# A two-layer graph attention kernel: the last chunk's pairs are taken one row later, its chain of small steps stays in the first twelve half pairs

## What is computed

```
h = relu(layernorm(x));  x = x + hyperbolic_graph_conv(h, adj)       # "L0_gnn"
h = relu(layernorm(x))
for beta in (beta1, beta2):                                           # "L1_gnn", two layers
    n = h / |h|
    s = where(adj > 0, beta * (n @ n.T), -1e9)
    h = leaky_relu(softmax(s) @ h)                                    # slope 0.3
x = x + h
```

## Time and profile before

| | before |
|---|---|
| median of 3 executions | 963.98 us (963.15 to 964.41) |
| the profiled execution, its own time | 963.64 us |
| span of its trace | 962.0 us |
| PE busy | 926.9 us, 96% of the span |
| PEld busy | 692.1 us, 72% |
| DVE busy | 792.5 us, 82% |
| ACT busy | 538.0 us, 56% |
| chain that ended last | PE 86%, ACT 6%, DVE 5% |
| DMA | 207.26 MB, mean 215 GB/s |

### The profile page before, as it was taken

How to read it: one execution, slowest core, us unless ns; L and a number is a source line. 1 busy time by engine, 2 the same in 40 slices (tenths; PEclk the granted TensorE clock), 3 DMA queues, 4 the chain that set the end, 5 groups by cost and what they waited for, 6 DMA issues and landing times.

```text
span 962.0 us, 22931 instructions
## 1 busy us (share of the span) xinstructions
PE 926.9 (96%) x9016; PEld 692.1 (72%) x9016; DVE 792.5 (82%) x1980; ACT 538.0 (56%) x867; POOL 7.2 (1%) x20
## 2 busy tenths in 40 slices
PE   7799999999997999999999999999999999999996
PEld 6644444444445878888888888778888888888886
DVE  7874778777789887978989898998788787888888
ACT  7802222232337766657656667796575565656564
POOL 0000000000000000000000000000000000000000
PEclk9999999999999999999999999999999999999998
DMA  8368888888851555455655545545455555565631
GB/s 298 154 222 289 283 298 293 279 286 283 293 180 57 232 196 210 186 202 198 249 195 212 220 180 216 210 160 201 177 219 219 232 206 201 220 228 194 259 144 37
DMA packets 30419, 207.26 MB, mean 215 GB/s; under 512 B 3632, under 2 KB 4784, under 8 KB 5744
## 3 DMA queue, kind: packets, MB, share of 16 engines
q1 hardware_dynamic: 28752, 203.70, 58.5%
q0 software_dynamic: 560, 1.84, 0.5%
q10 hardware_dynamic: 1008, 0.33, 0.1%
HBM read 203.75 MB, written 2.10 MB: 214 GB/s over the span
## 4 chain that ended last, share of the span: by engine, by line
PE 86%; ACT 6%; DVE 5%; issue 2%; DMA 0%; DVEq 0%; ACTq 0%
PE acc_ps L496 23%; PE s_ps L649 18%; PE s_ps L635 10%; PE acc_ps L707 6%; PE acc_ps L703 6%; PE acc_ps L705 6%; PE acc_ps L680 5%; PE acc_ps L676 5%; PE acc_ps L678 5%; ACT work L1078 1%; ACT set L800 1%; DVE work L1742 1%; PE s_ps L477 1%; ACT xt L822 1%; DVE work L1750 1%
## 5 line engine op out<-in xcount | busy, mean ns | idle before, releaser
L1078 ACT ACTIVATE work<-s_ps,beta_bias,beta_scale 128x1024 f32<-128x1024 f32 x144 | 173.5, 1205 | 212.2 <-PE s_ps L649 212.2
L496 PE MATMUL acc_ps<-ring,set 128*128 128x512 f32 x512 | 222.1, 592 | 1.6 <-DVE set L1348 1.6
L1760 DVE SCALAR_TENSOR_TENSOR h_all<-ring,s_ps 128x1024 f32<-128x1024 f32 x112 | 136.6, 1220 | 65.3 <-PE s_ps L635 63.9
L496 PEld LDWEIGHTS acc_ps<-ring,set 128*128 128x128 f32 x512 | 96.2, 190 | 117.5 <-issue 115.6
L1742 DVE TENSOR_TENSOR work<-work 128x1024 f16<-128x1024 f32 x96 | 132.7, 1382 | 5.4 <-ACT work L1088 5.4
L1088 ACT ACTIVATE work<-work 128x1024 f16<-128x1024 f32 x96 | 131.5, 1370 | 3.0
L1750 DVE SCALAR_TENSOR_TENSOR work<-ring,work 128x1024 f32<-128x1024 f32 x96 | 116.9, 1218 | 0.0
L649 PE MATMUL s_ps<-xt 128*128 128x512 f16 x432 | 105.4, 379 | 4.1 <-ACT work L1078 3.3
L649 PE MATMUL s_ps<-set 128*128 128x512 f16 x432 | 105.0, 379 | 0.5 <-ACT work L1078 0.5
L703 PE MATMUL acc_ps<-src,work 128*128 128x129 f16 x576 | 102.5, 219 | 2.0 <-DVE work L1750 2.0
L707 PE MATMUL acc_ps<-src,work 128*128 128x129 f16 x576 | 102.8, 222 | 0.0
(11 more groups left out here) (279 smaller groups left out, 1737.9 us busy)
## 6 DMA issues: line engine op xcount, KB each, us to landing
ring<-in_adj_t SPq DMA_DIRECT2D x192, 1024.0 KB, 5.0
x_sb<-in_x SPq DMA_DIRECT2D x4, 512.0 KB, 7.2
out<-x_sb POOLq DMA_DIRECT2D x7, 256.0 KB, 2.7
out<-x_sb SPq DMA_DIRECT2D x1, 256.0 KB, 2.7
w<-in_layer ACTq DMA_DIRECT2D x2, 64.0 KB, 8.2
w<-in_embed ACTq DMA_DIRECT2D x1, 64.0 KB, 4.5
eb<-in_embed_bias ACTq DMA_DIRECT2D x1, 64.0 KB, 6.9
lb<-in_layer_bias ACTq DMA_DIRECT2D x1, 64.0 KB, 7.9
```

Of the source, the lines that this page charges most:

```text
L496: last = nc.tensor.matmul(agg, v_sb[:, jb, :], ring[:, k, b, :], start=jb == 0, stop=jb == NB - 1)
L1078: nc.scalar.activation(values[x.n % VR], score_ps, ACT.Exp, bias=beta_bias[:, x.la:x.la + 1], scale=beta_scale[:, x.la:x.la + 1]).then_inc ...
L1760: V.scalar_tensor_tensor(turned[x.off % MR].rearrange("p (b j) -> p b j", b=CB), ring[:, x.mir_tile % AR, :, ds(x.h * HB * P, HB * P)], 0. ...
```

## The change

The order of the first layer's pairs becomes (0,0), ... (0,6), (1,1), ... (1,7), (7,0), (2,2), and then as before. Row 0 is thus left open after its first fourteen half pairs: its own sums are copied out to `mirror_sums` by a new ACT step (`own_kept`), row 1 is done (half pairs 14 to 27), and the missing pair is done as (7,0) (half pairs 28 and 29), where the rows of 7 are the "own" ones and those of 0 the mirrored. A new DVE step (`late_total`) makes row 0's total from the kept and the mirrored sum and adds the own part to what is kept for row 7. Before, row 0 ended at half pair 15 and row 1 at 29; now row 1 ends at 27 and row 0 at 29. Chunk 7's columns are turned at slot 24 instead of 12; the first half pair that needs them is 26 instead of 14. The column sums must wait until the bank of own sums is opened for row 1, and go to slots 18 to 23 and 27. `SLOTS_PER_PAUSE` is 1, so the chain of chunk 7 has its twelve pieces in the same slots 1 to 12 as before. The second layer's order is unchanged.

```
+        LATE = NC - 1
+        kept_seg = add_seg(0, 0, range(LATE), None, 0)
+        seg = add_seg(0, 1, range(1, NC), 0, 1)
+        rows_of.append(Row(0, 1, seg.first, seg.last))
+        late_seg = add_seg(0, LATE, (0,), None, 2)
+        rows_of.append(Row(0, 0, kept_seg.first, late_seg.last))
+        LATE_ROW = 1
...
-        LAST_CHUNK_AT = 12
-        turned_at = {LAST_CHUNK_AT: (0, NC - 1), **{rows_of[a].last + (11 if a == 5 else 10): (1, a) for a in range(NC)}}
...
+        LAST_CHUNK_AT = 24
+        order_of = {(r.la, r.a): i for i, r in enumerate(rows_of)}
+        turned_at = {LAST_CHUNK_AT: (0, NC - 1), **{r.last + (11 if r.a == 5 else 10): (1, r.a) for r in rows_of[:NC]}}
...
-        SUMS_AT_OF = {4: (0, 1), 5: (2,), 6: (3,), 7: (4,), 8: (5,), 14: (6,), SUMS_AT: (7,)}
...
+        SUMS_AT_LA = (rows_of[0].last, LAYER + 2 * NC - 1)
+        SUMS_AT_OF = {SUMS_AT_LA[0] - 11 + i: c for i, c in {2: (0, 1), 3: (2,), 4: (3,), 5: (4,), 6: (5,), 7: (6,),
+                                                             11: (7,)}.items()}
...
+        SLOTS_PER_PAUSE = 1
...
+                    if x.pair == late_pair:
+                        last = nc.tensor.matmul(mir_ps[:, x.h, o], tiny[:, :], sums_parts, start=False, stop=True)
...
-                if x.n == r.first and x.row != LAST_ROW:
-                    wait(pe, total_made, x.row)
...
+                if x.n == seg.first and seg.row != LAST_ROW:
+                    wait(pe, total_made, seg.opens_after)
...
+            def own_kept():
+
+                act.wait_ge(own_added, kept_seg.last + 1)
+                nc.scalar.activation(mirror_sums[:, 0:CB, :].rearrange("p (k b) w -> p k (b w)", k=2), own_ps, ACT.Copy)\
+                    .then_inc(total_made, 1)
...
+                if x.la == 0 and (x.a, x.b) == (1, NC - 1):
+                    V.tensor_copy(kept, mir_ps).then_inc(flushed, 1)
+                    return
...
+            def late_total():
...
+                dve.wait_ge(mir_added, half[late_seg.last].off + 1)
+                dve.wait_ge(total_made, 2)
+                dve.wait_ge(flushed, late_pair)
+                V.tensor_tensor(both, kept, mir_ps, ALU.add).then_inc(flushed, 1)
+                dve.wait_ge(own_added, late_seg.last + 1)
+                V.tensor_tensor(late, late, own_ps, ALU.add).then_inc(total_made, 1)
+                dve.wait_ge(flushed, late_pair + 1)
+                V.reciprocal(fin[:, LATE_ROW % 2, 0, :], sums_in[:, :, F]).then_inc(inverse_made, 1)
```

More of the change, by code:

```diff
@@ L290, in __call__ @@
                 self.eng.wait_ge(self.s, self.base + self.n)
-        Half = namedtuple("Half", "la a b h n off pair row own_tile mir_tile")
+        Half = namedtuple("Half", "la a b h n off pair seg own_tile mir_tile")
+        Seg = namedtuple("Seg", "first last row opens_after")
         Row = namedtuple("Row", "la a first last")
-        half, rows_of, tile_of = [], [], []
+        half, segs, rows_of, tile_of = [], [], [], []
         off_count = [0]
[L296 to L308, removed]
@@ new lines, in add_seg @@
+        def add_seg(la, a, bs, row, opens_after):
+            first = len(half)
+            for b in bs:
+                own_tile = len(tile_of)
+                tile_of.append((b, a, len(half) + 1, None))
+                if b != a:
+                    tile_of.append((a, b, len(half) + 1, off_count[0] + 1))
+                for h in range(2):
+                    off = off_count[0] if b != a else None
+                    off_count[0] += b != a
+                    half.append(Half(la, a, b, h, len(half), off, off // 2 if b != a else None, len(segs),
+                                     own_tile, own_tile + 1))
+            segs.append(Seg(first, len(half) - 1, row, opens_after))
+            return segs[-1]
@@ new lines, in build @@
+        LATE = NC - 1
[5 more added lines that the diff above has]
+        LATE_ROW = 1
+        for a in range(2, NC):
+            seg = add_seg(0, a, range(a, NC), a, a + 1)
+            rows_of.append(Row(0, a, seg.first, seg.last))
+        for a in range(NC):
+            seg = add_seg(1, a, range(a, NC), NC + a, NC + 1 + a)
+            rows_of.append(Row(1, a, seg.first, seg.last))
@@ L313, in build, with flushes_before, rows_summed_to, totals_to @@
         row_ending = {r.last: i for i, r in enumerate(rows_of)}
-        LAST_CHUNK_AT = 12
-        turned_at = {LAST_CHUNK_AT: (0, NC - 1), **{rows_of[a].last + (11 if a == 5 else 10): (1, a) for a in range(NC)}}
-        columns_before = {n: sum(m < n for m in turned_at) for n in turned_at}
-        SUMS_AT = 2 * NC - 1
-        SUMS_AT_OF = {4: (0, 1), 5: (2,), 6: (3,), 7: (4,), 8: (5,), 14: (6,), SUMS_AT: (7,)}
+        late_pair = half[late_seg.first].pair
+        def flushes_before(r):
+            return max([x.pair + 1 for x in half if x.off is not None and x.la == r.la and x.b == r.a], default=0)
+        def rows_summed_to(i):
+            return i + 1 - (i >= LATE_ROW)
+        def totals_to(i):
+            return i + 2
+        LAST_CHUNK_AT = 24
+        order_of = {(r.la, r.a): i for i, r in enumerate(rows_of)}
+        turned_at = {LAST_CHUNK_AT: (0, NC - 1), **{r.last + (11 if r.a == 5 else 10): (1, r.a) for r in rows_of[:NC]}}
+        columns_before = {n: sum(m < n for m in turned_at) for n in turned_at}
+        def turn_of(la, c):
+            return order_of[0, c] if la else c
+        SUMS_AT_LA = (rows_of[0].last, LAYER + 2 * NC - 1)
+        SUMS_AT_OF = {SUMS_AT_LA[0] - 11 + i: c for i, c in {2: (0, 1), 3: (2,), 4: (3,), 5: (4,), 6: (5,), 7: (6,),
+                                                             11: (7,)}.items()}
+        SUMS_AT_OF.update({LAYER + i: c for i, c in {4: (0, 1), 5: (2,), 6: (3,), 7: (4,), 8: (5,), 14: (6,),
+                                                     2 * NC - 1: (7,)}.items()})
         def tile_wait(eng, q):
@@ L680, in mirrored_sum @@
                         last = nc.tensor.matmul(mir_ps[:, x.h, o], w[:, WORD_LO, col], src[x.la][:, q, F:AW],
-                                                start=False, stop=ib == CB - 1)
+                                                start=False, stop=ib == CB - 1 and x.pair != late_pair)
+                    if x.pair == late_pair:
+                        last = nc.tensor.matmul(mir_ps[:, x.h, o], tiny[:, :], sums_parts, start=False, stop=True)
                 last.then_inc(mir_added, 1)
@@ L687, in own_sum @@
             def own_sum(x):
-                r = rows_of[x.row]
+                seg = segs[x.seg]
                 pe.wait_ge(own_made, x.n + 1)
@@ L701, in own_sum @@
                         col, q = ds(u * CH + ib * P, P), x.b * CB + x.h * HB + u
-                        opens = x.n == r.first and u == 0 and ib % 2 == 0
+                        opens = x.n == seg.first and u == 0 and ib % 2 == 0
                         nc.tensor.matmul(own_ps[:, ib // 2, ds(ib % 2 * PW, PW)], w[:, WORD_HI, col],
@@ L710, in own_sum @@
                 last.then_inc(own_added, 1)
-                if x.n == r.last:
+                if x.n == seg.last and seg.row is not None:
                     pe.wait_ge(sums_split, 4 * x.la + 4)
@@ L729, in columns_turned @@
                 la, c = turned_at[n]
-                rows = rows_n[c % 2] if la else t3
-                pe.wait_ge(xn_ready[la], c + 1)
+                rows = rows_n[turn_of(la, c) % 2] if la else t3
+                pe.wait_ge(xn_ready[la], turn_of(la, c) + 1)
                 pe.wait_ge(raised, n + 1)
@@ L747, in pairs @@
                         own_sum(done)
-                    if n % LAYER in SUMS_AT_OF and n < NH:
-                        for c in SUMS_AT_OF[n % LAYER]:
+                    if n in SUMS_AT_OF:
+                        for c in SUMS_AT_OF[n]:
                             rows_summed(n // LAYER, c)
@@ L1141, in slot @@
             def slot(n):
[L1142 removed]
+                if n - 1 in SUMS_AT_LA:
                     la = n // LAYER
@@ L1154, in slot @@
                 first = x and x.off is not None and x.h == 1 and x.a == 0
-                if i is not None and rows_of[i].a == 0:
+                own_leaves = n - 4 == kept_seg.last or (i is not None and i == NC)
+                if n - 4 == kept_seg.last:
+                    own_kept()
+                elif i == NC:
                     first_total(i)
@@ L1160, in slot @@
                     raise_scores(at(n))
-                if i is not None and first:
+                if own_leaves and first:
                     first_flush(x)
@@ L1174, in between @@
             def between(i):
-                slot(i + 1)
+                for n in range(SLOTS_PER_PAUSE * i + 1, SLOTS_PER_PAUSE * (i + 1) + 1):
+                    slot(n)
             def pairs():
                 last_chunk(between)
-                for n in range(PAUSES + 1, NH + 4):
+                for n in range(SLOTS_PER_PAUSE * PAUSES + 1, NH + 4):
                     slot(n)
@@ L1857, in slot @@
                 x = at(n - 4)
```

(13 more changed lines are left out.)

40 lines of the change are left out of this document (23 added, 17 removed).

## The result

| | before | after |
|---|---|---|
| median, 5 executions each | 963.16 us (962.91 to 964.41) | 967.51 us (967.32 to 968.31) |
| ratio after / before | | 1.0039, 95% interval 1.0027 to 1.0051 |
| the profiled execution, its own time | 963.64 us | 967.32 us |
| span of its trace | 962.0 us | 965.8 us |
| PE / PEld / DVE / ACT busy | 926.9 / 692.1 / 792.5 / 538.0 us | 926.7 / 691.2 / 793.8 / 537.8 us |

The account below looks back on a forecast made before the run. DVE, with ACT in slots 10 and 11, bounds slots 4 to 11; PE leads afterwards. Sums +2.7 and row ends +1.2 give +3.9 on 963.98: 967.9 us, own range 966.9 to 968.8, 8-in-10 range 965.6 to 969.8.

Parts of the forecast that it names:

- What bounds the kernel: Slots 4 to 11 lose 3.9 us; DVE bounds slots 4 to 9, DVE with ACT 10 and 11; PE leads afterwards.
- the 0.84: Slots 8 and 9: 0.84 us over PE's own work, put down to DVE.
- Part 1: Chunk 7's turn moved from slot 12 to 24: gain 0; the chain's pieces and the 3.9 us of stalls stay.
- Part 2: Six column sums leave slots 4 to 8, where DVE leads, for full slots 18 to 22: +2.7 us.
- Part 3: own_kept, open row, late pair: 0; row 1's total 2.0 us into slot 31, needed at 2.7, 0.7 to spare.
- Rival C: Slot 31's total over 0.7 us late, or row pieces of slots 34 to 38 add up: 970.4 us, chance 9%.
- Part 4: Two row ends interleave in slots 33 to 38: PE waits 0.9 us for ACT's exp, 0.3 for low halves, +1.2.
- 0.3 in slot 38: Slot 38: PE wants DVE's low halves at 27.4, they are done at 27.7, so it waits 0.3 us.
- The sum: Whole kernel: +2.7 + 1.2 = +3.9 us, on a median of 963.98 us.
- The signs: Slots 4 to 11 unmoved to 0.3 us, 18 to 22 longer, 12 at 4.93, idle before slot 35, 3.9 later from 40.
- A: PE led slots 4 to 8, so the stalls there dissolve without the sums: 961.3 us, chance 4%.
- B: Row-end cost hidden and half the sums' price got back in slots 4 to 8: +1.35, 965.3 us, chance 12%.

Follow-up runs that it names:

- the first experiment: The changed kernel with the column sums of chunks 0 to 5 issued in slots 4 to 8 again: 964.98 us, ratio 1.0013.
- the second: The kernel before, its order of pairs kept, with the first layer's column sums of chunks 0 to 5 in slots 12 and 13: 966.21 us, ratio 1.0028.
- flush-first run: The changed kernel with the first six small steps of row 0's scale moved behind the flush at the start of slot 37: 967.35 us, ratio 1.0035.
- first two runs: Column sums of chunks 0 to 5 early again in the changed kernel, 964.98 us; the same sums late in the kernel before, 966.21 us.
- two staggered versions: Changed kernel, chain pieces two slots apart, DVE's and ACT's pauses staggered: 961.69 us; the same with row 0's steps four slots later: 960.46 us.
- the staggered version: The changed kernel with SLOTS_PER_PAUSE = 2 and pauses no longer alike on DVE and ACT: 961.69 us, ratio 0.9981.
- the one with row 0 later: The staggered version with row 0's steps behind its total four slots later as well: 960.46 us, ratio 0.9966.
- first three experiments: Changed kernel with sums early, 964.98 us; kernel before with sums late, 966.21 us; changed kernel with chunk 7 turned at slot 12, 967.82 us.
- the other six: Changed kernel with: row 0 later, 966.90 us; flush first, 967.35; two-slot pauses, 967.83; staggered, 961.69; staggered and row 0 later, 960.46; that with sums early, 961.00.
- two-slot version: The changed kernel with SLOTS_PER_PAUSE = 2, chunk 7's twelve chain pieces two slots apart in slots 1 to 24: 967.83 us, ratio 1.0042.

## Why the prediction was right

- **What bounds the kernel.** PE doesn't lead slots 4 to 8. Shown: 48 matmuls could be taken out or put back with 0.1 us of effect on them, in both directions. That DVE is the one who leads there is read from the waits: 5.0 us of PE's idle time from 300 to 345 us stands ahead of transposes that wait for DVE's low halves. One small part of the 0.84 that I had put on DVE in slots 8 and 9 isn't DVE's: PE waits 0.19 in slot 9 for ACT's `first_flush`, in both traces.
- **Part 1, the deadline: 0.** Turned at 12 again, the same time within the measurement; the chain's pieces in DVE's and ACT's queues were the cost, not the date at which they had to be ready. That they kept their slots kept the stalls.
- **Part 2, the sums: +2.7.** Measured 2.6 late, 0.07 back early, so 2.5; 2.5 by the first experiment's trace, 2.4 (medians) to 2.7 (ratio) by the second's times. The slot that I had named as PE's, slot 5, gives back 0.07.
- **Part 3: 0.** Slots 30 to 33 take 5.16, 4.16, 4.16 and 3.54 us, which is their own work, and no wait for the total of row 1 appears. DVE has it done 2.03 us into slot 31 and PE's own sum starts 2.79 into it: 0.76 to spare, against a forecast of 2.0, 2.7 and 0.7. Rival C's first half (0.7 us to spare would not do) didn't happen.
- **Part 4: +1.2, measured 1.58.** ACT's part was forecast at 0.9 and came at 0.82, in the slot and for the reason named. The rest was mis-sized: I had 0.3 in slot 38, for the low halves, and the trace has 0.76 in slot 37. The step that was wrong is the one that let PE's `mirrored_sum` of slot 37 start when its mask was ready. It also waits for the flush of the pair before, which DVE has at the start of slot 37. By my own working DVE starts that flush at 19.3 and has it done at 19.9, while PE starts slot 37 at 18.0 and is through with its scores 1.3 later, at 19.3: a wait of 0.6, and the trace has 0.61. (It has slot 37 at 17.9 and the flush from 19.2 to 19.9, counted from the start of slot 33.) I had put the flush in DVE's sum but not asked who waits for it. The flush-first run shows that the low halves I had reckoned with come into sight (0.42 in slot 38) once the flush is out of the way.
- **The sum.** From slot 4 (0.39 us earlier than before) to the last scores (948.03 against 944.27) the trace of the change falls behind by 4.15 us; 2.5 + 1.58 = 4.1. The forecast was 3.9. The time came nearer than its parts: the sums were 0.2 too dear, part 4 was 0.4 too cheap, and the forecast stood on a median of 963.98 us for the kernel before, where the runs beside the result have 963.16. The first of these cancels half of the second, and that is luck.
- **The signs.** Slot 12 takes 4.93, the wait ahead of the scores of slot 35 is 0.66 and named after ACT's exp, slots 18 to 22 are longer as said, and from slot 40 on PE is 3.75 us later. One sign was missed: slots 5 to 11 start 0.4 to 0.5 us earlier than before, not within 0.3. Of this, 0.28 is there at slot 0 already, so it isn't an effect of the early slots.
- **Rivals.** A falls with the first two runs. B falls with the size of both terms. Of C only a beginning came: the row pieces do add up in slot 37, but part 4 is 1.58 and not 3.0. The time lies in the forecast's own range.

Two things I had not forecast lie outside the change: that a rest of one slot between the pieces, alike on both engines, gains nothing, and that the stagger of one slot then gains 6.1 us.

## What to carry to other kernels

- Work on an engine that waits is free where it stands and costs its length where the engine is full. Ask of each instruction that an edit moves off what covered it, and what it is put on.
- A chain that goes back and forth between two in-order engines is placed by its handshakes. Give the asking engine a slot of other work between the question and the answer, instead of equal rests on both; a later deadline alone buys nothing.
- In a sum over an overloaded engine, list for each of its results who waits for it. The wait shows at the first of them, and an edit that moves only that one passes it to the next.

## What was not expected of the hardware

The profiled executions of the two staggered versions, which have the same instructions on every engine up to slot 32, take 14.24 and 13.28 us from the scores of slot 2 to those of slot 5. The difference is the clock. Two stretches, the staggered version first, then the one with row 0 later (columns as in the earlier trace rows; the granted clock is the third number from the end, 1.00 is 2.4 GHz and 0.50 is 1.2 GHz):

```profile
289.00:297.00 8.00, 4.31 (x36) 2.46 (x36) 7.33 (x16) 7.23 (x8) 0.00 (x0) 1.00 0.01 2
297.00:301.00 4.00, 3.58 (x13) 2.32 (x14) 3.16 (x4) 0.00 (x0) 0.00 (x0) 0.57 0.37 104
```

```profile
289.00:297.00 8.00, 5.89 (x25) 2.78 (x26) 6.77 (x15) 6.34 (x7) 0.00 (x0) 0.60 0.01 2
297.00:301.00 4.00, 3.58 (x34) 2.68 (x33) 3.92 (x5) 1.59 (x3) 0.00 (x0) 0.95 0.25 41
```

In both, TensorE runs at its lower level for a few microseconds, but at different moments. In the first this meets slot 4, whose six score matmuls take 2.41 us instead of 1.46, and slot 4 takes 4.50 us instead of 3.71. In the second it is over before slot 4 and lies mostly in slot 3, where PE waits for DVE anyway. The traces of the kernel before, of the change and of the first three experiments have 1.00 in the whole attention stage; those of the other six have such a dip in slots 1 to 4. So a difference between two traces that arises in slots 1 to 4 is no proof of an edit's worth where a clock differs; the 1.4 us of slot 4 in the two-slot version stands, since the clock is at 1.00 in slot 4 of both traces.

The mean granted clock of a whole execution goes with its time, too. Of the 21 executions of the kernel before that stand beside the first experiments, the five with a mean granted clock of 0.996 or 0.997 took 962.98 to 963.41 us, the sixteen with a lower one 963.45 to 964.41. No run here shows what decides whether and when the clock falls.
